# Cross-attention and an 8-expert FFN on one core: the residual MLP in float32r parts, and q and k stacked from SBUF

## The reference

```
x = x + xattn(layernorm(x), ctx, ctx)      # 16 heads of 16, one shared k and v head
    q = layernorm(x) @ w_q ; k, v = concat(ctx, ctx) @ w_kv
    softmax(q k^T / 4) v  -> @ w_concat
y = layernorm(x)
x = x + y + ffn(y):
    a = layernorm(y) * nw + nb             # 2048 tokens x 256
    top-1 gate over 8 experts, capacity 256 tokens each, places by order of tokens
    moe  = gate weight * (gelu(a_e @ inter_w[e] + b) @ output_w[e] + b2)   # 256 -> 1024 -> 256
    res  = gelu(a @ res_inter_w + b) @ res_output_w + b2                   # the residual MLP
    out  = res * coef0 + moe * coef1 + y,  coef = softmax(a @ res_coef)
```

## Time and profile before

| | |
|---|---|
| time, median of 3 runs | 373.2 us (372.02 to 373.33) |
| profiled execution: its own time | 374.39 us |
| profiled execution: span of the core | 372.7 us |
| mean granted TensorE clock | 0.959 |
| busy: PE, PEld, DVE, ACT, POOL | 340.6, 277.6, 207.8, 217.9, 160.5 us |
| DMA | 49.83 MB, mean 134 GB/s |

### The profile page before, as it was taken

How to read it: one execution, slowest core, us unless ns; L and a number is a source line. 1 busy time by engine, 2 the same in 40 slices (tenths; PEclk the granted TensorE clock), 3 DMA queues, 4 the chain that set the end, 5 groups by cost and what they waited for, 6 DMA issues and landing times.

```text
span 372.7 us, 6349 instructions
## 1 busy us (share of the span) xinstructions
PE 340.6 (91%) x2234; PEld 277.6 (74%) x2234; DVE 207.8 (56%) x533; ACT 217.9 (58%) x397; POOL 160.5 (43%) x219
## 2 busy tenths in 40 slices
PE   3748889999999999999999989989999999999990
PEld 2425545875885885886786776778899999999990
DVE  4255528843762673574475462422668977878550
ACT  3311376484474465456447346363799999999730
POOL 4430233369657446636735542446002443334232
PEclk9965599999999999999999999999999999999996
DMA  6665539381224306706804400102936987875122
GB/s 183 197 202 144 166 106 315 117 230 60 79 82 116 99 28 179 261 2 176 288 2 133 107 2 15 44 1 66 295 84 182 279 272 189 233 199 140 17 30 28
DMA packets 51336, 49.83 MB, mean 134 GB/s; under 512 B 4765, under 2 KB 48489, under 8 KB 51305
## 3 DMA queue, kind: packets, MB, share of 16 engines
q1 hardware_dynamic: 48232, 45.21, 40.4%
q0 software_dynamic: 3072, 4.21, 6.1%
HBM read 33.65 MB, written 15.63 MB: 132 GB/s over the span
## 4 chain that ended last, share of the span: by engine, by line
PE 83%; DVE 5%; ACT 4%; issue 2%; DMA 2%; SPq 1%; POOL 1%; POOLq 0%; DVEq 0%
PE ubank L651 25%; PE mbank L833 16%; PE mbank L651 12%; PE mbank L646 4%; PE mbank L839 4%; PE mbank L840 4%; PE mbank L838 4%; PE pbank L736 4%; PE sbank L704 4%; PE sbank L726 4%; DVE smax L1069 2%; PE pbank L745 2%; DMA qstack<-dram_q 1%; DMA wq_raw<-in_L_xattn_w_q 1%; ACT h L976 1%
## 5 line engine op out<-in xcount | busy, mean ns | idle before, releaser
L976 ACT ACTIVATE h<-ubank,vecT 128x256 f32<-128x256 f32 x128 | 53.1, 467 | 29.8 <-PE ubank L651 29.7
L619 POOL DMA_INDIRECT out_rows<-yrow,rowid x16 | 32.3, 2017 | 74.0 <-DVE yrow L1213 74.0
L833 PE MATMUL mbank<-w2r,h 128*128 128x256 f32 x256 | 61.6, 383 | 1.5 <-ACT h L976 0.7
L651 PE MATMUL ubank<-ao,w1r 128*128 128x256 f32 x256 | 60.4, 382 | 0.0
L1069 DVE TENSOR_REDUCE smax<-sbank 128x4 f32<-128x512 f32 x64 | 42.5, 686 | 21.1 <-PE sbank L704 20.7
L833 PEld LDWEIGHTS mbank<-w2r,h 128*128 128x128 f32 x256 | 47.1, 190 | 9.3 <-issue 1.6
L651 PEld LDWEIGHTS ubank<-ao,w1r 128*128 128x128 f32 x256 | 46.8, 190 | 5.8
L910 ACT ACTIVATE p<-sbank 128x512 f32<-128x512 f32 x64 | 35.7, 596 | 15.7 <-PE sbank L726 15.5
L838 PE MATMUL mbank<-w2h,hh 128*128 128x256 f32 x128 | 36.4, 285 | 0.0
L840 PE MATMUL mbank<-w2h,hl 128*128 128x256 f32 x128 | 36.0, 281 | 0.0
L839 PE MATMUL mbank<-w2l,hh 128*128 128x256 f32 x128 | 36.0, 281 | 0.0
(11 more groups left out here) (139 smaller groups left out, 668.4 us busy)
## 6 DMA issues: line engine op xcount, KB each, us to landing
w1e<-in_L_ffn_inter_w SPq DMA_DIRECT2D x8, 1024.0 KB, 6.6
w2e<-in_L_ffn_output_w SPq DMA_DIRECT2D x8, 1024.0 KB, 7.9
qstack<-dram_q SPq DMA_DIRECT2D x16, 384.0 KB, 4.7
dram_q<-qpart SPq DMA_DIRECT2D x8, 384.0 KB, 2.6
dispatched<-zrow SPq DMA_DIRECT2D x4, 516.0 KB, 6.1
drow<-dispatched SPq DMA_DIRECT2D x8, 258.0 KB, 7.6
xs<-in_x SPq DMA_DIRECT2D x8, 256.0 KB, 3.2
ctxs<-in_ctx SPq DMA_DIRECT2D x8, 256.0 KB, 3.4
```

The source lines that it names most:

```text
L619: pool.indirect_dma_start(out=out[:, :], in_=yrow[:, e % 2, t, :], in_offset=None, compute_op=ALU.add, out_offset=bass.IndirectOffsetOnAxi ...
L651: last = nc.tensor.matmul(dst, w[kc], v[kc], start=(kc == 0), stop=(kc == len(w) - 1))
L833: last = nc.tensor.matmul(b[:, 0:D], h[:, n % 2, f, t * P:(t + 1) * P], w2[:, f, :], start=(f == 0), stop=(f == FC - 1))
L976: nc.scalar.activation(h[:, n % 2, f, :], place["up", n, c][:, j, :], ACT.Gelu_apprx_tanh, bias=vecT[:, col:col + 1]).then_inc(sem("gelu_d ...
```

## The change

1. The residual MLP is computed as the experts are, as MLP number -1: up and down take the three float32r products for all n. Its weights get low parts (w1rl, w2rl, in the place of w1r, w2r) and high parts (w1rh, w2rh), made by steps ws1(-1, q), ws2(-1, q) early in the program. ao, aoh and aol become separate and have two buffers; a new step low(u) on DVE makes aol for a unit, and ACT copies aoh and hh for all n.
2. The experts' buffers 0 and 1 (w1e, w2e, w1l, w2l) now lie in attention's region; buffer 2 is the residual's. Of the high parts w1h and w2h one buffer is new and one is the residual's. So expert 0 is loaded when the last unit's q and v are done and its stacks are in, expert 1 after x1_ready of the last unit, expert 2 when the residual MLP of the last unit has used its weights.
3. The DRAM tensors for q and k and the step gather are gone. kspill issues six DMAs from kpart into kstack, qspill 6, 4 and 2 DMAs from qpart into qstack, each of one part, one block of 16 rows and, for q, one batch. They wait for b_done of unit u - 2.
4. POOL counts the scaling of xs by a semaphore xs_scaled, and the bias step waits for it.
5. All places (OWN, AT0, AT1, AT, EXPERT, LOADS, all lags) have new numbers.

```diff
+        def mlp(n):
+            return max(n - U, -1)
+
+        def arrived(w, e):
+            return (f"{w}r_in", 16) if e < 0 else (f"{w}e_in{e % SETS}", 16 * (e // SETS + 1))
...
             def wload(e):
-                if e == 2:
+                if e == 0:
+                    sp.wait_ge(sem("q_done"), U)
+                    sp.wait_ge(sem("v_done"), U)
+                    for r in range(2):
+                        for t in range(T):
+                            sp.wait_ge(sem(f"q_in{r}{t}"), REP * 16 * U // 2)
+                        sp.wait_ge(sem(f"stack_in{r}"), REP * 16 * U // 2)
+                if e == 1:
                     sp.wait_ge(sem("x1_ready"), U)
...
-            def k_spill(u):
-                r = u % 2
+            def k_stack(u):
+                r, row = u % 2, 0
                 sp.wait_ge(sem("k_parts"), u + 1)
                 if u >= 2:
-                    sp.wait_ge(sem(f"stack_in{r}"), 16 * (u // 2))
-                row = 0
+                    sp.wait_ge(sem("b_done"), G * (u - 1))
                 for parts in (3, 2, 1):
-                    sp.dma_start(dram_k[r, row:row + parts].rearrange("a d t -> d a t"), kpart[:, r, 0:parts, :])\
-                      .then_inc(sem(f"k_spill{r}"), 16)
-                    row += parts
-
-            def q_spill(u, i):
+                    for i in range(parts):
+                        sp.dma_start(kstack[row:row + DH, r, :], kpart[:, r, i, :]).then_inc(sem(f"stack_in{r}"), 16)
+                        row += DH
+
+            def q_stack(u, i):
                 r, (name, row, times) = u % 2, (("q_hi", 0, 3), ("q_mid", 3, 2), ("q_parts", 5, 1))[i]
                 sp.wait_ge(sem(name), u + 1)
                 if u >= 2:
+                    sp.wait_ge(sem("b_done"), G * (u - 1))
+                for a in range(row, row + times):
                     for t in range(T):
...
+                        sp.dma_start(qstack[a * DH:(a + 1) * DH, r, t, :, :].rearrange("d (h m) x -> d h (m x)", m=KC),
+                                     qpart[:, r, i, t, :, :].rearrange("p m x -> p (m x)"))\
+                          .then_inc(sem(f"q_in{r}{t}"), 16)
...
             def up(n, c):
...
+                e = mlp(n)
+                if c == 0:
+                    pe.wait_ge(sem("ao_low"), n + 1)
+                    if n == 0 or n >= U:
+                        pe.wait_ge(sem("w1_low"), Q * (e + 2))
+                b = claim("up", n, c)
+                for j in range(2):
+                    f = slice((2 * c + j) * P, (2 * c + j + 1) * P)
+                    wh, wl = chunks(w1h[e % 2], f), chunks(w1l[e % SETS], f)
+                    ah, al = chunks(aoh[:, n % 2, :, :]), chunks(aol[:, n % 2, :, :])
+                    last = product(b[:, j, :], wh + wh + wl, ah + al + ah)
                 last.then_inc(sem("up_done"), 1)
 
             def down(n, t, q):
...
+                if t == 0:
+                    pe.wait_ge(sem("h_low"), C2 * n + q + 1)
...
+                    hi, lo = hh[:, n % 2, f, t * P:(t + 1) * P], hl[:, n % 2, f, t * P:(t + 1) * P]
+                    wh, wl = w2h[e % 2][:, f, :], w2l[e % SETS][:, f, :]
+                    nc.tensor.matmul(b[:, 0:D], hi, wh, start=(f == 0), stop=False)
+                    nc.tensor.matmul(b[:, 0:D], hi, wl, start=False, stop=False)
+                    last = nc.tensor.matmul(b[:, 0:D], lo, wh, start=False, stop=(f == FC - 1))
```

On ACT, the copy that every unit now has (before, experts alone), and on DVE the subtraction:

```diff
-                if n >= U:
-                    if n >= U + 2 and c == 0:
-                        act.wait_ge(sem("down_done"), T * (n - 1))
-                    act.wait_ge(sem("gelu_done"), 2 * (i + 1))
-                    copy(hh[:, n % 2, 2 * c:2 * c + 2, :], h[:, n % 2, 2 * c:2 * c + 2, :]).then_inc(sem("h_high"), 1)
+                act.wait_ge(sem("gelu_done"), 2 * (i + 1))
+                copy(hh[:, n % 2, 2 * c:2 * c + 2, :], h[:, n % 2, 2 * c:2 * c + 2, :]).then_inc(sem("h_high"), 1)
...
+            def low(n):
+                dve.wait_ge(sem("ao_high"), n + 1)
+                V.tensor_tensor(aol[:, n % 2, :, :], ao[:, n % 2, :, :], aoh[:, n % 2, :, :].bitcast(f32), ALU.subtract)\
+                    .then_inc(sem("ao_low"), 1)
```

The places, of which these decide the order in the middle:

```diff
-    PERIOD = 31.98
-    OWN = [0.0, 13.94, 43.2, 72.27]
+    PERIOD = 33.22
+    OWN = [0.0, 16.18, 49.6, 82.28]
...
+        "load": [-94.42], "ln1": [-96.73], "xn": [-45.76], "ctxT": [-51.06], "xT": [-42.78], "kv": [-51.06],
+        "q": [-39.02], "qrest": [-40.34], "qmid": [-46.62], "qlast": [-35.04], "vt": [-38.88],
+        "A": [-19.75, -19.37, -15.36, -14.88, -13.48, -11.07, -10.74, -8.34], "M": [-14.1, -7.63],
+        "B": [-1.96, -1.03, 3.71, 4.82, 7.97, 9.0, 10.62, 11.81], "PV": [11.62, 14.3], "part": [14.58, 16.81],
+        "o": [13.03, 13.11], "oT": [17.89], "proj": [21.99], "ln2": [18.96], "core": [25.76], "low": [31.85],
+        "gate": [31.28], "loc": [37.91], "gw": [5.05], "bias": [-76.23], "up": [19.16, 24.17, 25.22, 27.0],
+        "down": [-0.62, 0.55, 1.72, 2.35, 5.02, 6.37, 8.44, 10.49], "kspill": [-7.28],
+        "qspill": [-33.61, -32.09, -31.28],
...
+        "core": [1.93], "gate": [3.68], "loc": [3.45], "A": [-1.46], "B": [-1.62], "PV": [-1.42], "part": [-0.79],
+        "up": [-0.64], "down": [-1.39], "oT": [0.33], "proj": [0.0], "M": [-0.06], "q": [1.03], "kv": [2.32],
+        "vt": [0.03], "xT": [0.42], "ctxT": [0.3], "ein": [-8.02], "vec": [1.84],
```

More of the change, by code:

```diff
@@ L82, in xattn_moe_ffn_kernel @@
-        "qspill": [-33.14, -29.81, -29.17], "gather": [-40.06, -39.06],
+        "load": [-95.14], "ln1": [-94.87], "xn": [-45.44], "ctxT": [-51.14], "xT": [-39.47], "kv": [-51.35],
+        "q": [-38.92], "qrest": [-45.27], "qmid": [-47.17], "qlast": [-49.57], "vt": [-37.65],
[3 rows of a table added]
+        "gate": [35.09], "loc": [46.22], "gw": [4.0], "bias": [-77.3], "up": [19.62, 23.62, 24.44, 26.19],
+        "down": [-0.98, 6.31, 7.62, 9.28, 9.44, 14.98, 15.68, 19.27], "kspill": [-7.28],
+        "qspill": [-34.33, -32.51, -31.69],
@@ L104, in xattn_moe_ffn_kernel @@
+        "small": [0.0], "ws2": [-4.8],
     }
     LAG_DVE = {
-        "core": [-0.6], "gate": [0.07], "loc": [0.0], "A": [0.0], "gw": [-2.85], "o": [-0.98], "proj": [-0.12],
-        "M": [0.24], "vt": [0.0], "ln1": [0.85], "ln2": [0.1], "down": [-0.19], "ein": [0.11], "qrest": [-4.34],
-        "small": [0.0], "vec": [0.0], "up": [1.48], "ws2": [-0.56], "xn": [-1.24], "qlast": [0.27], "ws1": [1.13],
+        "core": [-0.49], "gate": [7.06], "loc": [2.48], "A": [-1.42], "gw": [3.11], "o": [2.22], "proj": [0.0],
@@ L113, in xattn_moe_ffn_kernel @@
+        "down": [-2.21], "qlast": [-4.47], "end": [1.88], "small": [0.0], "ws1": [1.57],
     }
     LAG_SP = {
-        "load": [-4.81], "kspill": [-5.64], "qspill": [-0.35], "gather": [13.54], "M": [3.71], "wload": [0.2],
-        "ein": [1.22], "down": [7.99], "zero": [3.09], "late": [0.29], "w1load": [-0.02], "end": [-0.43],
-        "small": [0.55], "w2load": [0.66],
+        "load": [-23.3], "kspill": [-31.36], "qspill": [-4.1], "M": [-7.82], "wload": [0.44], "ein": [-13.71],
+        "down": [1.02], "zero": [-1.91], "late": [-31.81], "w1load": [-0.81], "end": [0.82], "small": [0.0],
@@ L140, in xattn_moe_ffn_kernel @@
         for kind in ("load", "ln1", "xn", "ctxT", "xT", "kv", "q", "qrest", "qmid", "qlast", "vt", "oT", "proj", "ln2",
-                     "core", "gate", "loc"):
+                     "core", "low", "gate", "loc"):
             if kind != "load" or u >= 2:
@@ L147, in xattn_moe_ffn_kernel @@
             add(max(OWN[u] + phase, free + 0.1 * (i + 1)), "qspill", u, i)
-        for i in range(T):
-            add(max(OWN[u] + at["gather"][i], free + 0.5 + 0.1 * i), "gather", u, i)
         for i in range(T - HALVES[u], T):
@@ L164, in xattn_moe_ffn_kernel @@
         add(LOADS["zero"][b], "zero", b)
-    for e, (own, phase) in enumerate(zip((0, 3, 4, U - 1), LOADS["weights"])):
+    for e, (own, phase) in enumerate(zip((0, U - 1, U - 1), LOADS["weights"])):
         add(OWN[own] + phase, "wload", e - 1)
-    for e in range(E):
+    for kind in ("ws1", "ws2"):
+        for q, phase in enumerate(LOADS[kind]):
+            add(OWN[0] + phase, kind, -1, q)
+    for e in range(-1, E):
         own = OWN[U + 1] + EXPERT["period"] * (e + 1)
+        if e + SETS < E:
+            for kind in ("w1load", "w2load"):
+                add(own + EXPERT[kind][0], kind, e + SETS)
+        if e < 0:
+            continue
         add(OWN[U + 1] + EXPERT["first"][0] if e == 0 else own - EXPERT["ein"][0], "ein", e)
@@ L176, in xattn_moe_ffn_kernel @@
                 add(own + phase, kind, e, q)
-        if e + SETS < E:
-            for kind in ("w1load", "w2load"):
-                add(own + EXPERT[kind][0], kind, e + SETS)
     add(1e6, "end")
@@ L494, in end @@
                 sp.wait_ge(sem("acc_out"), 16 * (NBATCH + 1))
[L496 removed]
```

(1 more changed line is left out.)

228 lines of the change are left out of this document (83 added, 145 removed), and 18 rows, old and new, of tables (AT, AT0, AT1).

## The result

The changed kernel takes 384.67 us (median of 4 runs, 380.56 to 385.49); the kernel before took 373.26 us beside it. The ratio is 1.0264, interval 1.0156 to 1.0371: slower, where 360.3 us and faster were forecast. The profiled execution has a span of 382.8 us against 372.7.

A forecast was written before the change was run, and what follows sets the result against it. TensorE's own work was taken as the bound: -19.8 us (residual MLP), +4.9 (waits for core and stacks), +1.0 (start), +1.0 (passage to experts) gave -12.9, so 360.3 us against 373.2; range 352.5 to 369.

The forecast's parts named there:

- Stacks straight from SBUF: Direct q and k copies between q and the scores: 0.3 us wait; with core's 0.5, 4.9 us over seven units.
- the term for the start: First units: splitting the residual weights on ACT and DVE not fully hidden, +1.0 us, between -2 and +4.
- The formula, 12p - 6.8 us: Wait before a unit's scores, p being SP's time per q issue: 0.3 us at the 0.59 us taken.
- Rival 3: SP late with the stacks: 4.4 us wait a unit at 0.93 us an issue, 381.8 us; chance 0.13.
- the passage to the experts: From the last unit to the first expert: routing chain and ACT's split copies not fully covered, +1.0 us.
- that cancels: At the start: unit 1's DMAs land a microsecond or two late, but unit 0's B steps fill it; no cost.
- Rival 4: Residual MLP's float32r products come at 0.108 us each: 27.7 us saved, 345.5 us; chance 0.03.
- rival 2: Residual MLP's downs wait for the new operands hh and hl once a unit: 366 to 372 us; chance 0.14.
- Ports: Copies of 64 KB into 16 neighbouring rows reach few DMA ports: 0.6 us of data each, sum unchanged.

The follow-up runs named there:

- Run 5: Changed kernel with k's stack filled by three DMAs a unit instead of six, k's rows reordered, q's twelve kept: 367.98 us, ratio 0.9890 to the kernel before.
- Run 3: Changed kernel with 24 extra small bf16 products ahead of the wait for the stacks of units 2 to 7: 380.57 us.
- run 6: Changed kernel with both merges, q in six DMAs and k in three, nine issues a unit: 359.33 us, ratio 0.9611 to the kernel before.
- run 8: run 6's kernel with the dispatched rows of experts 1 to 3 loaded right behind expert 0's: 356.77 us.
- run 9: Kernel before with the direct stacks alone, q's and k's copies merged (nine issues a unit), old places, residual MLP float32: 370.03 us, ratio 0.9911.
- run 7: run 2's kernel with 20 extra products per unit in the residual MLP, 18.9 us of TensorE in all: 380.74 us, 12.7 us more.
- run 10: run 8's kernel with the same 20 extra residual products per unit, 18.9 us of TensorE in all: 371.43 us, 14.7 us more.
- run 1: Changed kernel with q and k sent through DRAM again, nine DMAs a unit: 375.27 us, ratio 1.0085 to the kernel before.
- run 4: Kernel before with the direct stacks alone, eighteen copies a unit, old places, residual MLP float32: 391.60 us, ratio 1.0508.
- run 2: Changed kernel with q's copies merged over both batches, six DMAs a unit instead of twelve: 368.04 us, ratio 0.9862 to the kernel before.

## Why the prediction was wrong

**The step that failed is "Stacks straight from SBUF", and with it the term for the start**, where the same issues were taken to cancel. The stacks are late behind SP's queue, 2.1 us (mean) ahead of the scores of units 2 to 7 where 0.3 was taken, and far more is lost at the start. To divide the miss, I count the records of the residual MLP by their times: 86 of 512 passes lie ahead of M(3) before, 139 of 768 products after. The sum's terms come then, as an estimate, to about +1 us by M(3), -7 over the next four units and -6 in the tail. Measured were +14.0, -0.4 and -3.5. So of some 23 us of miss in the span, 13 are at the start, 6 to 7 in the four units, and 2 to 3 in the tail.

**The wait in a steady unit.** The formula, 12p - 6.8 us, had the right mechanism and rested on three sizes. Measured at A(5,0), from the moment q's first part is copied: k's issues ahead of q add 0.62 us of delay, which the formula didn't have at all, though it knew of six issues for k. Twelve issues take 8.33 us, p = 0.69 with the gaps (0.64 without), not 0.59. Both together make 8.95 us where 7.1 was taken. The scores start 1.4 us after the last issue, where 1.9 was taken for the landing, and PE was ready 8.3 us after the copy, not 8.7. So the wait is 8.95 + 1.39 - 8.28 = 2.06 us, not 0.3. Rival 3, SP late, is what happened. It was priced by p alone, with a deciding point of 0.84 us; with k's issues and the clock counted the point lies lower. Run 5, which takes three of k's issues away and brings the kernel below the one before, shows that k's issues count. Rival 3's time, 381.8 us, came near the measured one by luck: it has 26.4 us of waits in six units and 2 us for the start and the passage to the experts; the six measured waits sum to 12.6 us, and the start lost most.

**The clock was not in the sum.** Run 3 prices its falls at 4.1 us by the medians, 2 to 5 by the other measures. Ahead of A(5,0) that is a wait of 2.06 us and then the next products 0.5 us slower (PV 1.53 for 0.99), and more behind them; ahead of A(4,0) a longer wait, 2.53 us, had no fall behind it.

**The start** was taken as +1.0 us, between -2 and +4. It lost 14.0 us by M(3), although part of the residual work lies ahead of that already. The step "that cancels" was wrong: 12 of unit 1's 18 issues stand ahead of the first half of unit 0's maxima in the same queue, and the other six ahead of the second half. SP's timeline of the changed kernel there:

```profile
12.99 7.72 SPq L472 DMA_DIRECT2D qstack<-qpart  x12
20.75 3.75 SPq L462 DMA_DIRECT2D kstack<-kpart  x6
...
25.69 3.67 SPq L462 DMA_DIRECT2D kstack<-kpart  x6
29.41 3.79 SPq L472 DMA_DIRECT2D qstack<-qpart  x6
33.24 1.23 SPq L484 DMA_DIRECT2D qstack<-nmax  x2
```

The first half's maxima go out at 33.24 us, 27.56 before. First scores were forecast at 23.9 us by 18 issues at 0.5; at 0.64 they started at about 25.7. Then the loss grows: it is 4.5 us at M(1), 9.5 at M(2) (81.9 for 72.4) and 14.0 at M(3). Behind M(1) unit 2's eighteen copies go out from 53.7 to 65.8 us, and the chain waits for the last of them:

```profile
64.57 2.59 DMA qstack<-qpart
67.16 0.09 issue
67.25 0.61 PE sbank L715 x8
```

Before, unit 2's first scores start at 59.77 us. With both merges M(3) comes at 102.5.

**What held.** The residual MLP and the experts are 24 products in 2.83 us, 0.118 each, as in the earlier trace rows; the chain of the changed kernel:

```profile
293.13 2.83 PE ubank L662 x24
304.94 2.83 PE ubank L662 x24
```

The experts come every 11.8 us. Rival 4 is out: 0.108 us is nowhere. By the Trainium skill's page "FP8 and Floating Point Precision" (TensorE Precision Notes) three passes for four would have given 27.7 us; the row's 0.118 decides. PE's waits for hl are 1.2 us in the whole span, so rival 2 is out too, and ACT and DVE rose only to 64% and 61% of the span (58% and 56% before). The tail gained 3.5 us where about 6 were forecast, and it is no shorter in run 6 (148.5 us), whose stacks are in time; where the rest went is open. The stores of residual rows that held up expert 1's rows, an issue order I hadn't looked at, turned out free in run 8.

**How large the gain was.** With the stacks in time (run 6) the kernel takes 359.33 us and the mean unit 26.6, where the forecast said 360.3 and 27.0 to 27.3. That doesn't make the working right. Of it 3.9 us is the gain of the direct stacks at the start (run 9), which the sum had as a cost, and by runs 7 and 10 extra residual work costs 0.67 to 0.78 of PE's time for it; if taking work away counts as much, that is 13 to 15 us and not 19.8. The parts also don't add: residual parts with DRAM are 2.1 us slower than before (run 1), direct stacks with nine issues 3.9 faster (run 9), and both 14.1 faster (run 6). My reading is that a shorter residual MLP also shortens the time in which the stacks must arrive, so that it pays only with a shorter path from q to the stacks; the waits of run 1 (2.22 us) and run 6 (none) fit it. It isn't shown. Runs 4 and 9 have the places of the kernel before, the others those of the changed kernel, and neither the new places nor the residual parts at the old places were run alone, so what the places do isn't separated.

**Ports.** The prediction's estimate from the Trainium skill's page "SBUF — State Buffer" (Door 1: The DMA port swizzle), 0.6 us of data for a copy of 64 KB into 16 rows, isn't contradicted. Into 16 neighbouring rows copies of 64 KB landed in 2.7 us (changed kernel) and copies of 128 KB in 4.3 (run 2); with the row order of runs 5 and 6, which spreads a copy's 16 rows over up to 48, it was 2.2 and 3.3 us. In the changed kernel this wasn't the limit, since half as many copies of twice the size were faster. In run 2 the transfer was what the scores waited for, with the DMA engines busy for 0.98 of the time. The spread rows fit as the reason why run 6 had half of that; since k's merge came with them, that stays open.

## What to carry to other kernels

Count DMA issues, all of them, by the queue that they stand in, and follow that queue to the first thing that waits behind them: here three issues of 0.62 us a unit, for copies of 8 KB, were worth 16.7 us, 13.4 of them at the start. Before taking a tensor apart into many small copies, look for an order of its rows or columns in which one DMA does it, and look at the landing again when it does: with q merged alone, it was the larger copies' transfer that PE waited for. A saving on the busiest engine shortens the cover of every transfer beside it; re-work those distances with the saving in, and price a wait of some 2 us on TensorE with the clock that may fall behind it.

## What the runs showed of the hardware

Copies from SBUF to SBUF were issued every 0.62 us for 8 KB (3.69 us for six) and every 0.64 us for 64 KB (7.66 us for twelve). Those of 128 KB took 0.63 to 0.64 us each where SP didn't wait for data (1.88 us for three at the start of run 6), and k's three merged copies of 24, 16 and 8 KB, over 48, 32 and 16 rows, 1.88 us together. So twice or three times the data cost nothing at the issue here. At the landing it did: 2.7 us for 64 KB and 4.3 for 128 KB into 16 neighbouring rows, 2.2 and 3.3 with the rows spread.

After waits of 2.00 to 2.22 us on TensorE the granted clock of the next ten microseconds read 0.68 to 0.83 in the changed kernel (four waits); after one of 2.53 us and one of 1.56 it read 1.00, and so it did after 0.97 us with k merged. So the length of the wait alone doesn't tell whether the clock falls. With 24 small products in the wait it stayed at 1.00 in the two stretches shown.
